# The last two blocks of the normalised x turned over by DMA instead of by TensorE

## What is computed

```
h = relu(layernorm(x))                       # 1250 x 1024
e = sigmoid(h @ wenc.T + benc)               # 1250 x 500, the "encoder"
h2 = e @ conv_weight                         # 1250 x 500
agg = segment_sum(h2[src] * edge_weight, dst)
x = x + (agg + e @ lin_weight.T) @ wdec.T + bdec
h = relu(layernorm(x))                       # second layer: a normalised
x = x + gcn(h, edges, W, b)                  # graph convolution, 1024 -> 1024
```

## Time and profile before

| | |
|---|---|
| time, median of 3 runs | 473.05 us (472.91 to 473.27) |
| the profiled execution's own time | 473.33 us |
| its span in the trace | 471.5 us |
| TensorE matmuls busy | 465.3 us, 99% |
| VectorE busy | 314.1 us, 67% |
| ScalarE busy | 203.2 us, 43% |
| GpSimd busy | 35.3 us, 7% |
| DMA, mean rate over the span | 149 GB/s |

### The profile page before, as it was taken

The page is one execution under the profiler, slowest core; times in us unless marked ns, Lnnn a source line. Parts: engine busy times, 40 slices in busy tenths (PEclk is TensorE's granted clock), DMA queues, the critical chain, the costliest instruction groups (busy, mean ns, idle before and its releaser), DMA issues.

```text
span 471.5 us, 9281 instructions
## 1 busy us (share of the span) xinstructions
PE 465.3 (99%) x3496; PEld 405.8 (86%) x3496; DVE 314.1 (67%) x608; ACT 203.2 (43%) x408; POOL 35.3 (7%) x36
## 2 busy tenths in 40 slices
PE   7999999999999999999999999999999999999997
PEld 6999999978878888889888888888889988888886
DVE  5989886687857852594758787839351646566652
ACT  6985684655542222222535544547352622222220
POOL 3300000000000000000000000365500000000000
PEclk9999999999999999999999999999999999999999
DMA  7720124292123670538540004261969316546542
GB/s 304 260 81 24 67 69 141 81 349 77 67 67 67 123 263 2 113 110 310 188 161 1 0 2 172 97 264 48 385 241 371 125 22 246 200 178 224 181 177 104
DMA packets 37663, 70.26 MB, mean 149 GB/s; under 512 B 16844, under 2 KB 25694, under 8 KB 35954
## 3 DMA queue, kind: packets, MB, share of 16 engines
q1 hardware_dynamic: 37298, 69.24, 42.3%
q0 software_dynamic: 320, 0.39, 0.4%
HBM read 44.33 MB, written 22.01 MB: 141 GB/s over the span
## 4 chain that ended last, share of the span: by engine, by line
PE 92%; DVE 5%; DMA 1%; ACT 1%; issue 0%; POOL 0%; SPq 0%; DVEq 0%; ACTq 0%; POOLq 0%
PE bank L1330 23%; PE bank L1331 22%; PE bank L1332 22%; PE bank L1346 18%; PE bank L1443 2%; DVE stats L985 2%; PE bank L1445 1%; PE bank L1447 1%; PE bank L1463 1%; DVE we L569 1%; DMA h<-x 1%; DVE h0T L1081 0%; DVE wc L569 0%; DVE wd_lo L569 0%; ACT wd_hi L829 0%
## 5 line engine op out<-in xcount | busy, mean ns | idle before, releaser
L1346 PE MATMUL bank<-a,h_hi 128*128 128x256 f16 (+3 forms) x400 | 85.5, 270 | 0.0
L1346 PE MATMUL bank<-a,h_lo 128*128 128x256 f16 (+3 forms) x400 | 85.5, 270 | 0.0
L1330 PE MATMUL bank<-right,left 128*128 128x512 f32 (+1 forms) x148 | 56.0, 378 | 0.0
L1331 PE MATMUL bank<-right,left 128*128 128x512 f32 (+1 forms) x148 | 55.9, 378 | 0.0
L1332 PE MATMUL bank<-right,left 128*128 128x512 f32 (+1 forms) x148 | 55.9, 378 | 0.0
L1315 DVE SCALAR_TENSOR_TENSOR x<-bank,dis_u,x 128x512 f32<-128x512 f32 (+2 forms) x37 | 26.7, 722 | 38.7 <-PE bank L1332 38.5
L949 ACT CAST left<-zs 128x512 fp32r<-128x512 f32 x35 | 21.7, 624 | 64.3 <-PE bank L1332 64.3
L1330 PE MATMUL bank<-unit,g 128*128 128x500 f32 (+3 forms) x120 | 42.3, 353 | 0.4 <-DVE unit L1187 0.4
L1346 PEld LDWEIGHTS bank<-a,h_hi 128*128 128x128 f16 (+1 forms) x400 | 39.0, 97 | 4.2 <-issue 0.3
L1346 PEld LDWEIGHTS bank<-a,h_lo 128*128 128x128 f16 (+1 forms) x400 | 39.1, 98 | 3.7
L1332 PE MATMUL bank<-unit,g 128*128 128x500 f32 (+3 forms) x120 | 42.2, 352 | 0.0
(11 more groups left out here) (152 smaller groups left out, 1105.0 us busy)
## 6 DMA issues: line engine op xcount, KB each, us to landing
right_scratch<-right SPq DMA_DIRECT2D x5, 2048.0 KB, 8.6
right<-right_scratch SPq DMA_DIRECT2D x5, 2048.0 KB, 7.7
whole<-w SPq DMA_DIRECT2D x7, 1024.0 KB, 7.5
adj_scratch<-stage SPq DMA_DIRECT2D x50, 125.0 KB, 1.8
raw<-adj_scratch SPq DMA_DIRECT2D x2, 2500.0 KB, 9.3
h<-x SPq DMA_DIRECT2D x9, 512.0 KB, 6.1
x<-x SPq DMA_DIRECT2D x9, 512.0 KB, 5.9
out<-x SPq DMA_DIRECT2D x18, 256.0 KB
```

The source lines that it names most:

```text
L1330: pe.matmul(o, lhs[0], rhs[0], start=first, stop=False, skip_group_check=True)
L1331: pe.matmul(o, lhs[0], rhs[1], start=False, stop=False, skip_group_check=True)
L1346: ins = pe.matmul(o, h1[i][0:n, k, 128 * f:128 * (f + 1)], moving, start=(k == 0 and part == 0 and i == 0), stop=(k == T - 1 and part == p ...
```

## The change

For the blocks 3 and 4 (tiles 6 to 9; `BY_DMA = 3`) TensorE no longer transposes. ScalarE makes the relu twice per tile, once in 16 bits (`x16`, high part) and once in 32 (in place); a new VectorE step `split` subtracts the 16-bit one and writes the rest in 16 bits; a new step `turn` on SP's queue issues two DMA transposes per tile, 128 x 1024 each, into `h16T`. The steps `t` and `lo t` of these blocks copy from `h16T` (SBUF) into `h0T` in place of reading a PSUM bank. So that the low part keeps its bits in 16 bits, rstd and nbias of these tiles are multiplied by 1024, and the sigmoids divide by it.

(lo t(2,2) stands behind e(1,1), lo t(2,3) behind e(1,2); the four lo t3 stand from t3 to behind e(2,3).) The diff, cut to its core:

```diff
@@ schedule()
     def norms(b):
-        return [("norm", 2 * b), ("norm", 2 * b + 1)]
+        pair = (2 * b, 2 * b + 1)
+        return [(n, t) for n in (("norm", "split", "turn") if b >= BY_DMA else ("norm",)) for t in pair]
...
     for b in range(1, NB):
         eb = encoder(b)
-        dense += eb[:1] + (turn(b + 1) if b + 1 < NB else [])
+        if b + 1 < BY_DMA:
+            dense += eb[:1] + turn(b + 1)
+            eb = eb[1:]
         if b == NB - 2:
             dense += [("load", "wc")]
         if b + 2 < NB:
-            dense += mix(eb[1:], statistics(b + 2) + norms(b + 2))
+            dense += mix(eb[:2], statistics(b + 2) + norms(b + 2)) + (turn(b + 1) if b + 1 >= BY_DMA else []) + eb[2:]
         elif b + 1 < NB:
-            dense += eb[1:]
+            dense += eb[:2] + turn(b + 1) + eb[2:]
         else:
-            dense += eb[1:2] + mix(eb[2:], cut_wc)
+            dense += eb[:2] + mix(eb[2:], cut_wc)
@@ build(): banks are given to ("t", b, q) only where b < BY_DMA
@@ SP
+                elif s[0] == "turn":
+                    t = s[1]
+                    b, j = divmod(t, 2)
+                    sp.wait_ge(split_ready, t - 2 * BY_DMA + 1)
+                    if b > BY_DMA:
+                        hi_done(sp, ("t", b - 1, KD // 2 - 1))
+                        read_done(sp, ("t", b - 1, KD // 2 - 1))
+                    else:
+                        acc_done(sp, ("edges",))
+                    for i in range(2):
+                        sp.dma_start(h16T[:, i, :, P * j:P * (j + 1)], x16[t % 2][:, i, :], transpose=True).then_inc(turned[t], 16)
...
                 elif s == ("load", "wc"):
-                    acc_done(sp, ("t", NB - 1, KD // 2 - 1))
+                    sp.wait_ge(split_ready, T - 2 * BY_DMA)
@@ ScalarE, norm
                     act.wait_ge(rstd_ready, t // 2 + 1)
+                    if t >= 2 * BY_DMA:
+                        if t >= 2 * BY_DMA + 2:
+                            act.wait_ge(turned[t - 2], 32)
+                        nc.scalar.activation(x16[t % 2][0:n, 0, :], h0[t % XRING][0:n, :], ACT.Relu, bias=nbias[0:n, t:t + 1],
+                                             scale=rstd[0:n, t:t + 1])
                     nc.scalar.activation(h0[t % XRING][0:n, :], h0[t % XRING][0:n, :], ACT.Relu, bias=nbias[0:n, t:t + 1],
                                          scale=rstd[0:n, t:t + 1]).then_inc(relu_ready, 1)
@@ ScalarE, t
+                    if by_dma(s):
+                        for t in (2 * b, 2 * b + 1):
+                            act.wait_ge(turned[t], 32)
+                        nc.scalar.copy(h0T[b % 2][0][:, 2 * q:2 * q + 2, 0:n], h16T[:, 0, 2 * q:2 * q + 2, 0:n]).then_inc(hi_ready, 1)
+                        continue
@@ VectorE
+                elif s[0] == "split":
+                    t = s[1]
+                    n = tile_rows(t)
+                    dve.wait_ge(relu_ready, t + 1)
+                    if t >= 2 * BY_DMA + 2:
+                        dve.wait_ge(turned[t - 2], 32)
+                    v.tensor_tensor(x16[t % 2][0:n, 1, :], h0[t % XRING][0:n, :], x16[t % 2][0:n, 0, :],
+                                    ALU.subtract).then_inc(split_ready, 1)
@@ VectorE, lo t
+                    if by_dma(s):
+                        for t in (2 * b, 2 * b + 1):
+                            dve.wait_ge(turned[t], 32)
+                        v.tensor_copy(h0T[b % 2][1][:, 2 * q:2 * q + 2, 0:n], h16T[:, 1, 2 * q:2 * q + 2, 0:n]).then_inc(bank_free, 1)
+                        continue
@@ TensorE
-                elif s[0] == "t":
+                elif s[0] == "t" and not by_dma(s):
```

More of the change, by code:

```diff
@@ L57 @@
 HSCALE = 1024.0
+BY_DMA = 3
+XSCALE = 1024.0
 MAGIC = 12582912.0
@@ L117, in agg_cols, with by_dma @@
     return min(S, NODES - S * n)
+def by_dma(s):
+    return s[0] == "t" and s[1] >= BY_DMA
 def schedule():
@@ L294, in build @@
         elif s[0] in ("t", "e", "g", "z", "edges"):
-            bank_for(s, *dense)
+            if not by_dma(s):
+                bank_for(s, *dense)
         elif s[0] == "o":
@@ L309, in build @@
             for g in [s] if parts is None else [(*s, i) for i in range(parts)]:
-                accs[g] = len(accs)
+                if not by_dma(g):
+                    accs[g] = len(accs)
                 if s[0] in ("s", "p", "o"):
@@ L415, in build @@
         firsts = at("firsts", [EP, ROWS], F16, R_RAW + 11008)
+        x16 = [at(f"x16_{i}", [P, 2, D], F16, R_RAW + 11776 + 4096 * i) for i in range(2)]
+        h16T = at("h16T", [P, 2, KD, B], F16, R_RAW)
         before = at("before", [EP, HC, ROWS], F16, R_C)
@@ L522, in build @@
         relu_ready = sem("relu_ready")
+        split_ready = sem("split_ready")
+        turned = {t: sem(f"turned{t}") for t in range(2 * BY_DMA, T)}
         wl_used = sem("wl_used")
@@ L632, in _ @@
                     sp.wait_ge(stage_ready, NW)
-                elif s[0] == "t" and s[2] == KD // 2 - 1:
+                elif s[0] == "turn":
[9 more added lines that the diff above has]
+                        sp.dma_start(h16T[:, i, :, P * j:P * (j + 1)], x16[t % 2][:, i, :], transpose=True).then_inc(turned[t], 16)
+                elif s[0] == "t" and s[2] == KD // 2 - 1 and not by_dma(s):
                     acc_done(sp, s)
@@ L676, in _ @@
                             sp.wait_ge(stage_out[i], 16 * len(range(i, WS, STG)))
+                        hi_done(sp, ("t", NB - 1, KD // 2 - 1))
+                        read_done(sp, ("t", NB - 1, KD // 2 - 1))
                     load_raw(n, raw_in[n])
@@ L846, in _ @@
                         act.wait_ge(bias_rows, 2)
+                    unscale = 1.0 / XSCALE if b >= BY_DMA else 1.0
                     nc.scalar.activation(hT[0][0:m, f, B * b:B * b + n], bank[banks_of[s]][0:m, 0:n], ACT.Sigmoid,
-                                         bias=benc_c[0:m, f:f + 1])
+                                         bias=benc_c[0:m, f:f + 1], scale=unscale)
                     nc.scalar.activation(sig[0:m, i, 0:n], bank[banks_of[s]][0:m, 0:n], ACT.Sigmoid,
-                                         bias=benc_c[0:m, f:f + 1]).then_inc(sig_ready, 1)
+                                         bias=benc_c[0:m, f:f + 1], scale=unscale).then_inc(sig_ready, 1)
                 elif s[0] == "g":
@@ L1026, in _ @@
                     dve.wait_ge(power_ready, t0 // 2 + 1)
-                    link(v.scalar_tensor_tensor(q, y, -0.5, y, ALU.mult, ALU.mult))
+                    times = XSCALE if t0 >= 2 * BY_DMA else 1.0
+                    link(v.scalar_tensor_tensor(q, y, -0.5 * times, y, ALU.mult, ALU.mult))
                     link(v.tensor_tensor(q, q, var, ALU.mult))
-                    link(v.scalar_tensor_tensor(rstd[:, t0:t1], q, 1.5, y, ALU.add, ALU.mult))
+                    link(v.scalar_tensor_tensor(rstd[:, t0:t1], q, 1.5 * times, y, ALU.add, ALU.mult))
                     v.scalar_tensor_tensor(nbias[:, t0:t1], mv[:, t0:t1, 0], -1.0, rstd[:, t0:t1], ALU.mult, ALU.mult).then_inc(rstd_ready, 1)
```

## The result

| | before | after |
|---|---|---|
| time, median | 473.29 us (472.91 to 473.45) | 483.15 us (482.48 to 485.01) |
| the profiled execution's own time | 473.33 us | 482.89 us |
| its span | 471.5 us | 481.0 us |
| TensorE transposes | 80 | 48 |
| DMA transposes of x | 0 | 8 |

The changed kernel takes 1.0213 times as long (95% interval 1.0203 to 1.0223): 9.9 us more. The forecast was 7.75 us more, 480.8 us.

A forecast was written before the change was run, and what follows sets the result against it. TensorE, busy 99% at full clock, was taken as the bound. Walking the engines' queues in the new order ("the walk") gave 11.0 us of new waits less 3.25 saved: +7.75, 480.8 us; own range 478.5 to 483, 8-in-10 range 477.2 to 487.0.

The forecast's parts named there:

- rival 1: TensorE's clock falls in the two 4 us waits: 3.9 us more each, 484.7 with one drop, 488.6 with both; chance 0.20.
- Wait 1: Before window 2: TensorE waits 4.0 us because four ScalarE relus of block 3 stand before window 0's read.
- Wait 2: Before window 8: TensorE waits 4.3 us for window 6's read, behind four ScalarE relus of block 4.
- Windows 6, 7, 10 and 11: TensorE waits 0.3, 0.55, 0.3 and 0.55 us there for one hots late on VectorE.
- Window 14: Starts about 0.8 us late: stores of windows 8 to 11 stand behind block 4's DMA transposes on SP's queue.
- Small: Further 0.2 us of waits for windows 3, 9 and 15, each 0.06 behind its neighbour's read.
- The split, the copies, the relu: Durations assumed for added work: split 1226 ns, 16-bit relu 1242 ns, VectorE copy 0.45 us, ScalarE copies 0.4 to 0.6.
- Transposes removed: On TensorE, blocks 3 and 4: 1.70 and 1.55 us of transposes that nothing hides, 3.25 us saved.
- The rule on transposes: Skill's 1309 ns per DMA-transposed tile, 390 on TensorE; eight tiles in turn take 10.5 us, total 485.3.
- Rivals 2 to 4: The first of these: SP's queue slower, 3.16 us a transpose, stores 7.3 us later, 488; chance 0.05.
- rival 3: Block 3's and 4's norms find ScalarE idle early enough, all waits gone: 469.8 us; chance 0.05.
- Rival 4: Same mechanism, smaller: copies at 0.3, issues at 1.07, splits at half price: +4.9, 478.0; chance 0.06 with below.

The follow-up runs named there:

- the new order alone: The change's step order only, against the kernel before: blocks 3 and 4 transposed by TensorE, one relu per tile, no split or turn; 476.23 us, ratio 1.0067.
- With the clock held: The whole change plus 32 unused TensorE matmuls ahead of window 2 and 36 ahead of window 8; 482.21 us, ratio 1.0198 to the kernel before.
- the spaced order: The whole change with a handwritten step list, one 16-bit and one 32-bit relu between each two evictions; 471.04 us, ratio 0.9959 to the kernel before.
- its control: The spaced order with TensorE's transposes for blocks 3 and 4, one relu, no split, no turn; 474.10 us, ratio 1.0019 to the kernel before.
- The block 4 kernel: The change with only block 4 turned over by DMA (`BY_DMA = 4`); 478.32 us, ratio 1.0109 to the kernel before; run again 477.55 us, 1.0099.

## Why the prediction was right, and where it was off by parts

The sign, the mechanism and the two places were right: ScalarE's relus in a row stood in front of a window's read, twice. The time came out 2.35 us above the forecast, inside the range. In part that is luck: the prediction's own sign of rival 1, a granted clock below 1 after 49 us, appeared, and the time stayed near only because both drops ran into waits that swallowed them, which the prediction had not foreseen. Term by term:

**Wait 1, 4.0 us.** Measured 3.81. The norms began at 42.85 for 43.0 and window 0's second read ended at 48.78 for 49.0. The kernel with the new order alone, two relus instead of four, had 1.50: the wait goes with the number of relus in the row.

**Wait 2, 4.3 us.** Measured 3.58 net of what came before; ScalarE began the second burst at 59.71 for 59.9, window 8 started at 65.68. The walk's starts hold; the wait is shorter only because TensorE arrived later. With the clock held it was free at 61.69 for the walk's 61.7 and started window 8 at 65.75, 4.06 later.

**Windows 6, 7, 10 and 11, 1.7 us together.** Not in the trace of after: there TensorE came 1.4 us late from the dropped clock and the one hots were ready. With the clock held, three of them appear, 0.17, 0.41 and 0.41, so the mechanism is shown and the size was too high.

**Window 14, 0.8 us.** Measured 1.86, the one term that was clearly too small. The queue time was right: 5.47 us for four transposes, 1.33 each at the median, for 4 x 1.34. What failed is the step "the store of 8 lands 2.1 later (0.33 and 1.8)": it landed 3.66 later. The median of fifty stores, none of which had a DMA transpose in front, was used for one right behind four transposes. Without block 4's transposes the wait is gone, so the cause is shown; why the landing is long is not.

**Small, 0.2, and the 0.5 us after window 16.** The small term is not separated. The 0.5, spread over 396 us, belongs to that one execution: in the second one it is gone, 395.7 us from window 16 to the end, as before.

**The split, the copies, the relu.** Split 1220 ns for 1226. The 16-bit relu 1234 for 1242. The copy on VectorE 407 ns, 0.34 from start to start, for the 0.45 taken between bounds of 0.3 and 0.6. ScalarE's copy was above its range, 656 ns for 0.4 to 0.6, and moved nothing. The transposes of block 3 landed 3.3 us after issue, well before they were wanted.

**Transposes removed, 3.25.** 32 matmuls fewer; the steps behind them moved up by 1.70 and 1.55. In the spaced order the net gain in the total was 3.06 against its control, and 2.1 against the kernel before.

**Rival 1, the clock.** It was given a chance of 0.20, and it happened at both places. It was left out of the sum with the reason that the clock was full in all slices of before; but that trace had no wait of this kind in the stretch, and a full clock in a stretch without waits says nothing of what happens behind one. It was priced at 3.9 us a drop, as if a step and two windows all ran at 1.2 GHz. The clock rose again halfway through the step, so the price was 1.44 and 1.49. And it was added to the waits, where in truth the first drop ran into wait 2 and the second into the wait of window 14, and both vanished there. The forecast was nearer than its parts: with the drops left out (the kernel with dummy matmuls), window 14 was 8.1 later than before where the walk has 7.7. There the store landed as the walk had it, 2.12; in the change it took 3.66, and window 14 was 8.9 later.

The Trainium skill ("TensorE: Matmul & The Clock Gate", section "Why this matters for your kernels") warns that gaps between bursts throw the clock back. The trace agrees: after all seven waits of 3.3 us or more that these runs have without dummies, the clock fell. It fell behind three of the five between 2.0 and 2.8 us as well. By that rule, at the measured price, the sum would have been 7.75 + 2.9 = 10.7, and 483.8. That this is nearer to the 483.15 measured does not bear the sum out: the 2.9 did not reach the total, and the store's landing did.

**The rule on transposes.** The Trainium skill ("VectorE: DVE Perf Modes", section "The three transpose paths") gives 1309 ns for one tile, which as an estimate made a transfer of eight tiles 10.5 us. The transfers landed after 3.3 us at the median, 0.41 a tile, and kept SyncE's queue for 1.33. The measurement decides: tiles of one transfer do not follow one another at that figure. The advice of the same page of the Trainium skill (section "Rules for kernel authors"), TensorE where a destination in PSUM will do, was not borne out in the spaced order, where DMA won by 3.06 us; in the order of the change it was.

**Rivals 2 to 4.** The queue was not slower (1.37 us the longest). The gain of rival 3 did not come from this order, and its condition, relus that find ScalarE idle and no eviction behind them, is what the spaced order makes: 471.0 where it put 469.8. Rival 4 fell on two of its three conditions: the copies came near its 0.3 (0.34), but the issues took 1.33 for its 1.07, and the splits 1220 ns, their full price.

## What to carry to other kernels

An operation taken off the engine that sets the time is worth its time only if what it brings to the other engines is put between their evictions; count how many of them stand in a row in front of the read that frees a bank. Where TensorE has no slack, count on the clock behind a wait of over 3 us too: 1.4 to 2.6 us were lost to it here each time. They reach the total (1.7 us in the one kernel where it could be seen) unless the next wait is set by another engine, which then swallows them. Before dropping a change that moved work off the bound and lost, run its two halves apart: here the order lost 3.0, the DMA path in that order 6.9 more, and in another order it gained 3.1 against the same order without it.

## What the runs showed of the hardware that was not expected

**A wait's length does not settle whether the clock falls.** Behind waits of 3.3 us and more it fell in seven of seven; behind 1.4 to 1.9 us (between 45 and 85 us of the span) in none of six; behind 2.00 to 2.29 it fell twice and held twice, once each way at the same window of the same kernel (2.01 and 2.03 us); behind 2.74 it fell. The loss ranged from 1.3 to 2.6 us.

**Matmuls without use hold it.** 33 of them in a wait of 3.6 us: clock 1.00 behind it, 1.67 us less in the total. In the change itself 32 and 36 held it too, and nothing of that is shown to have reached the total.

**The start is not always the same.** Between 10 and 15 us the granted clock was 1.00 in some executions, 0.66 or 0.73 in three and 0.50 in two. Of these two, TensorE was 0.8 us late at window 2 in one (45.85) and not in the other (45.09), so the clock record alone does not explain it. Nor does a record of 1.00 there settle the pace: the sixteen transposes from about 11 us on took 3.35 us in the profile of before at a recorded 1.00, 3.67 with block 4 by DMA and dummies at 0.50, and 2.23 with the new order alone at 1.00. Why is not shown. The block 4 kernel's two medians, 478.32 and 477.55, differ by as much as that late start; so a difference of under 1 us between kernels measured at different times isn't read as theirs here.

**Stores of 125 KB behind DMA transposes.** The first store behind four of them landed after 2.9 to 3.8 us in seven executions and after 2.1 in two, against 2.0 behind four plain copies and 1.8 at the median before.
